# Attention on one core: the products of probabilities and values on half arrays, one step later

## The reference, cut to what matters

```
def _gqa(q, k, v):
    scale = 1.0 / np.sqrt(q.shape[-1])
    scores = jnp.einsum('bsghd,btgd->bghst', q, k) * scale
    p = jax.nn.softmax(scores, axis=-1)
    return jnp.einsum('bghst,btgd->bsghd', p, v)
```

## Time and profile before

| | |
|---|---|
| median of 3 runs (lowest, highest) | 1151.28 us (1149.92, 1151.87) |
| the profiled execution, its own time | 1148.86 us |
| its span, first to last instruction | 1147.0 us |
| self attention, first to last matmul of the stage | 282.3 to 645.7 us |
| cross attention, the same | 662.1 to 1058.7 us |
| busy share of the span | PE 78%, PEld 72%, DVE 79%, ACT 65%, POOL 34% |

### The profile page before, as it was taken

The page is one execution under the profiler, slowest core; times in us unless marked ns, Lnnn a source line. Parts: engine busy times, 40 slices in busy tenths (PEclk is TensorE's granted clock), DMA queues, the critical chain, the costliest instruction groups (busy, mean ns, idle before and its releaser), DMA issues. The chain is left out here.

```text
span 1147.0 us, 22788 instructions
## 1 busy us (share of the span) xinstructions
PE 898.3 (78%) x6366; PEld 820.7 (72%) x6366; DVE 909.2 (79%) x2442; ACT 746.6 (65%) x2599; POOL 393.1 (34%) x500
## 2 busy tenths in 40 slices
PE   3720066621999999999999379999999999997738
PEld 3620033321899999999999269999999999996627
DVE  7989989877788888888888458888888888886461
ACT  3445034363888888888888457777777777775303
POOL 0008910000244444444443543333334333333024
PEclk9855569755999999999999789999999999999559
DMA  6021200001100000000000210000000000000400
GB/s 223 1 92 57 72 0 1 0 0 64 48 2 1 0 0 0 0 0 0 0 0 0 79 50 5 6 10 5 5 5 5 9 5 5 0 0 1 152 19 19
DMA packets 18265, 26.94 MB, mean 23 GB/s; under 512 B 1264, under 2 KB 15408, under 8 KB 17456
## 3 DMA queue, kind: packets, MB, share of 16 engines
q1 hardware_dynamic: 17840, 25.41, 6.5%
q0 software_dynamic: 384, 1.05, 0.3%
HBM read 23.83 MB, written 2.62 MB: 23 GB/s over the span
## 5 line engine op out<-in xcount | busy, mean ns | idle before, releaser
L1208 POOL TENSOR_TENSOR c_cat<-c_tb,c_mb 128x512 fp32r<-128x512 bf16 x64 | 74.7, 1167 | 228.9 <-DVE c_tb L1286 228.9
L1208 POOL TENSOR_TENSOR s_cat<-s_tb,s_mb 128x512 fp32r<-128x512 bf16 x64 | 74.3, 1161 | 178.6 <-DVE s_tb L1286 178.6
L1384 ACT ACTIVATE c_p<-c_kT_sc_ps,c_nmax 128x64 f32<-128x64 f32 x256 | 76.8, 312 | 79.4 <-DVE c_nmax L1252 79.4
L1384 ACT ACTIVATE s_p<-s_kT_sc_ps,s_nmax 128x64 f32<-128x64 f32 x256 | 76.8, 312 | 39.6 <-DVE s_nmax L1252 39.6
L1401 PE MATMUL s_q_ps<-wq,s_xqf 128*128 128x512 f32 x256 | 76.7, 422 | 32.9 <-POOL s_xqf L1190 32.9
L1401 PE MATMUL c_q_ps<-wq,c_xqf 128*128 128x512 f32 x256 | 76.8, 423 | 16.4 <-DVE wv L645 16.4
L1455 PE MATMUL s_pj_ps<-wp,s_cat 128*128 128x256 f32 x512 | 77.7, 294 | 2.9 <-POOL s_cat L1208 2.9
L1455 PE MATMUL c_pj_ps<-wp,c_cat 128*128 128x256 f32 x512 | 77.2, 293 | 2.9 <-POOL c_cat L1208 2.9
L1245 DVE TENSOR_REDUCE c_v<-c_sq 128x6 f32<-128x768 f32 x64 | 61.0, 953 | 16.2 <-ACT c_sq L1355 15.1
L1401 PEld LDWEIGHTS s_q_ps<-wq,s_xqf 128*128 128x128 f32 x256 | 44.3, 193 | 39.2 <-POOL s_xqf L1190 33.3
L1479 PEld LDWEIGHTS s_kT_sc_ps<-s_kT,s_qT 128*128 128x128 f32 x512 | 66.6, 191 | 7.4 <-ACT s_qT L1360 1.4
(11 more groups left out here) (361 smaller groups left out, 2985.0 us busy)
## 6 DMA issues: line engine op xcount, KB each, us to landing
x_res<-in_x SPq DMA_DIRECT2D x4, 512.0 KB, 5.4
vT<-in_ctxT SPq DMA_DIRECT2D x2, 1024.0 KB, 9.9
tf_work<-in_wqT SPq DMA_DIRECT2D x2, 1024.0 KB, 6.2
tf_work<-in_wprojT SPq DMA_DIRECT2D x2, 1024.0 KB, 5.4
w_work<-in_wqxT SPq DMA_DIRECT2D x2, 1024.0 KB, 6.6
w_work<-in_wkvxT SPq DMA_DIRECT2D x2, 1024.0 KB, 8.1
c_ctx<-in_ctxT SPq DMA_DIRECT2D x16, 128.0 KB, 2.3
w_work<-in_wprojT SPq DMA_DIRECT2D x2, 1024.0 KB, 5.7
```

Source lines behind the costliest of these rows:

```text
L1208: nc.gpsimd.tensor_tensor(cat[out8.o % 2][:], tb[:], mb[:], ALU.subtract).then_inc(cat_ready, 1)
L1384: nc.scalar.activation(pe_s[:, a * S:(a + 1) * S], sc_ps[:, a * S:(a + 1) * S], ACT.Exp, bias=nmax[:, a:a + 1], accum_out=psum_s[:, a:a + ...
```

## The change

The products with the values are computed for each sequence by itself. `pT` now holds only the blocks themselves (128 partitions x 256), written by one copy. For each group and each sequence, one matmul contracts over the 64 partitions of that sequence, 128 columns wide; partitions 0 to 63 lie on one half of the array's rows, 64 to 127 on the other. The two sequences write into two PSUM banks. No bank is free for that: a tensor `qo_ps` of three banks now holds, in its outer banks, the two query buffers, and in its middle one the old `po_ps`; the products of a unit go to the middle bank and to one of its neighbours (`out_banks`). So they wait until the normalised queries have been read out of that neighbour (`qn_ready` at pv.n + 3), and the queries that are next written there wait until the products have been read (`y_ready`).

The step of these products is one later on PE (unit u-4 instead of u-3), and the orders within a step change on PE, DVE and ACT. One constant of the first stage (`K_BOUND`, the value in a shift of exponents) is another number; it changes no instruction.

```
-        pT = sb("pT", [P, GU, HPG, 2, S])
+        pT = sb("pT", [P, GU * P])
-        q_ps = [psum(f"q_ps{i}", [P, QW]) for i in range(2)]
+        qo_ps = psum("qo_ps", [P, 3, 512])
+        q_ps, po_ps = [qo_ps[:, 2 * i, :] for i in range(2)], qo_ps[:, 1, :]
-        po_ps = psum("po_ps", [P, 512])
+        def out_banks(u):
+            return qo_ps[:, u.o % 2:u.o % 2 + 2, 0:HU * S]
@@ @block.gpsimd @@
-                nc.gpsimd.memset(pT[:], 0.0).then_inc(cleared, 1)
@@ @block.vector, step @@
+                    if f8.live:
+                        round8(3)
                     if sm.live:
                         maxima()
-                    if f8.live:
-                        round8(3)
                     if u.live:
                         normalised()
+                    if pv.live:
+                        dve.wait_ge(pv_done, pv.count(1, 1))
...
+                        nc.vector.tensor_tensor(yb[:].rearrange("p (h b s) -> p h b s", h=HU, b=2),
+                                                out_banks(pv).rearrange("p b (h s) -> p h b s", h=HU),
...
                     if sm.live:
                         dve.wait_ge(exp_ready, sm.count(4, 4))
                         wait_unit(dve, pn_ready, sm.before(1))
                         nc.vector.reciprocal(rsum[:], psum_s[:]).then_inc(rsum_ready, 1)
-                    if pv.live:
...
@@ @block.scalar, step @@
-                    u, sm, pv = units(i, o, 0, 1, 2)
+                    q, u, sm, pv = units(i, o, 0, 1, 2, 3)
...
-                        for b in range(2):
-                            rows = slice(b * S, (b + 1) * S)
-                            nc.scalar.activation(pT[rows, :, :, b, :], po_ps[rows, 0:GU * P].rearrange(
-                                "p (g h s) -> p g h s", g=GU, h=HPG), ACT.Copy).then_inc(pT_ready, 1)
+                        nc.scalar.activation(pT[:], po_ps[:, 0:GU * P], ACT.Copy).then_inc(pT_ready, 1)
...
+                    if q.live:
+                        act.wait_ge(q_done, q.count(1, 1))
+                        wait_unit(act, var_ready, q.before(1))
+                        nc.scalar.activation(sq[:, 0:QW], q_bank(q), ACT.Square).then_inc(sqq_ready, 1)
@@ @block.tensor, step @@
-                    u, kv_u, t, pv, pj = units(i, o, 0, 1, 2, 3, 5)
+                    u, kv_u, t, pt, pv, pj = units(i, o, 0, 1, 2, 3, 4, 5)
...
+                    if pv.live:
+                        pe.wait_ge(pT_ready, pv.count(1, 1))
+                        pe.wait_ge(qn_ready, min(pv.n + 3, UNITS) if pv.static else pv.count(1, 3))
+                        for g in range(GU):
+                            for b in range(2):
+                                rows = slice(b * S, (b + 1) * S)
+                                last = nc.tensor.matmul(out_banks(pv)[:, b, g * P:(g + 1) * P],
+                                                        v_s[pv.o % 4][rows, g * D:(g + 1) * D],
+                                                        pT[rows, g * P:(g + 1) * P], start=True, stop=True)
+                        last.then_inc(pv_done, 1)
...
+                        wait_unit(pe, y_ready, u.before(4))
...
-                        for g in range(GU):
-                            last = nc.tensor.matmul(po_ps[:, g * HPG * P:(g + 1) * HPG * P],
-                                                    v_s[pv.o % 4][:, g * D:(g + 1) * D],
-                                                    pT[:, g].rearrange("p h b s -> p (h b s)"), start=True, stop=True)
-                        last.then_inc(pv_done, 1)
```

More of the change, by code:

```diff
@@ L1084, in attention_stage @@
     ROUNDS = NT // 2
+    UNITS = WIDTH * ROUNDS
     QW, KW = HU * D, GU * D
@@ L1386, in step @@
                                                  ).then_inc(exp_ready, 1)
-                pipeline(act, step, ROUNDS, WIDTH, 2)
+                pipeline(act, step, ROUNDS, WIDTH, 3)
             @block.tensor
@@ L1438, in step @@
                         last.then_inc(tq_done, 1)
-                        pe.wait_ge(kn_ready, t.count(1, 1))
-                        wait_unit(pe, kT_ready, t.before(1))
-                        wait_unit(pe, exp_ready, t.before(1, 4))
-                        for a in range(GU):
-                            last = nc.tensor.transpose(kT_ps[:, a * P:(a + 1) * P], kn[:, a * P:(a + 1) * P], ident[:])
-                        last.then_inc(t_done, 1)
                     if pj.live:
@@ L1459, in step @@
                         last.then_inc(pj_done, 1)
-                    if pv.live:
-                        pe.wait_ge(pn_ready, pv.count(1, 1))
-                        wait_unit(pe, y_ready, pv.before(1))
-                        for g in range(GU):
-                            last = nc.tensor.transpose(po_ps[:, g * P:(g + 1) * P], pn[:, g * P:(g + 1) * P], ident[:])
-                        last.then_inc(pt_done, 1)
+                    if t.live:
+                        pe.wait_ge(kn_ready, t.count(1, 1))
+                        wait_unit(pe, kT_ready, t.before(1))
+                        wait_unit(pe, exp_ready, t.before(1, 4))
+                        for a in range(GU):
+                            last = nc.tensor.transpose(kT_ps[:, a * P:(a + 1) * P], kn[:, a * P:(a + 1) * P], ident[:])
+                        last.then_inc(t_done, 1)
                     if u.live:
@@ L1470, in step @@
                         wait_unit(pe, qn_ready, u.before(2))
-                        split_product(q_bank(u)[:], lambda h: xqf[tp][:, h, :], wq, gp * QW, (gp + 1) * QW
+                        wait_unit(pe, y_ready, u.before(4))
+                        split_product(q_bank(u), lambda h: xqf[tp][:, h, :], wq, gp * QW, (gp + 1) * QW
                                       ).then_inc(q_done, 1)
+                    if pt.live:
+                        pe.wait_ge(pn_ready, pt.count(1, 1))
+                        wait_unit(pe, y_ready, pt.before(1))
+                        for g in range(GU):
+                            last = nc.tensor.transpose(po_ps[:, g * P:(g + 1) * P], pn[:, g * P:(g + 1) * P], ident[:])
+                        last.then_inc(pt_done, 1)
                     if t.live:
```

26 lines of the change are left out of this document (8 added, 18 removed).

## The result

| | before | changed |
|---|---|---|
| median (lowest, highest) | 1150.95 us (1149.92, 1151.87), 4 runs | 1182.38 us (1179.81, 1185.25), 4 runs |
| the profiled execution, its own time | 1148.86 us | 1184.29 us |
| its span | 1147.0 us | 1182.6 us |
| mean step, self attention | 5.453 us | 5.785 us |
| mean step, cross attention | 5.907 us | 6.051 us |

The changed kernel takes 1.0274 times as long, 95% interval [1.0244, 1.0304]: 31 us slower. The prediction was 1174.5 us, range 1138 to 1222, with 0.74 for slower.

A forecast was written before the change was run, and what follows sets the result against it. PE's own work was taken to set the step before the change. Self attention +24.3, cross attention +0.6 and POOL's clearing -0.5 made +24.4 us; on 1148.86 that is 1173.3, with half of 2.4 added 1174.5 us, range 1138 to 1222.

The forecast's parts named there:

- The new wait: PE's products wait for DVE's qn of the unit two ahead, which puts them in series with DVE's step.
- Side by side: Products on the two array halves overlap, the second half starting one record late: 0.55 us, between 0.44 and 0.88.
- p: Time of the products with the values a step: 0.55 + 0.15 = 0.70 us, ends 0.54 and 1.08, against 0.92 before.
- The way back: PE's switch from 64 rows back to 128 after the products: 0.15 us, between 0.10 and 0.20.
- the first loop: Self attention: from qn through products, yb, s_r, tb and maxima back to qn; 5.07 us + p with the x_res addition.
- the second loop: Self attention: ACT's ln and exp behind kT, behind PE's moved key transposes; 5.16 us + p with the x_res addition.
- Self attention: Step 5.12 + 0.70 = 5.82 us against 5.44: +0.38, times 64 = +24.3 us.
- Cross attention: Step 5.92 us against 5.91, with 0.10 for the statistics: +0.6 us in all.
- 1: Rival: the array halves take turns, p = 1.03, self step 6.15, cross 6.25; 1217 us; chance 0.28.
- 2: Rival: the products halve to p = 0.46 and the switches vanish in the waits; 1144 us, faster; chance 0.08.
- 3: Rival: the loops are shorter than their parts and PE stays the bound; 1121 or 1136 us; chance 0.10.
- 4: Rival: it comes out even, p = 0.54 to 0.60 and a fixed part 0.1 shorter; within 0.2%; chance 0.08.

The follow-up runs named there:

- e1: Changed kernel with its new orders, but whole-array products into the old middle bank alone and without the two bank waits; 1150.47 us, 0.9993 of before.
- e2: e1 with the changed kernel's two bank waits (on qn_ready and y_ready) kept; 1213.74 us, 1.0552 of before.
- e8: Changed kernel, second sequence's products in the transposed queries' bank; PE does queries before transposes, ACT copies kT before qT; 1158.70 us, 1.0060 of before.
- e5: Changed kernel with both groups' products of the lower array half written ahead of those of the upper half; 1182.72 us, 1.0271 of before.
- e3: Changed kernel with PE's transposes of the keys right behind those of the queries, ahead of the projection; 1169.51 us, 1.0172 of before.
- e10: Changed kernel with DVE's addition into x_res moved behind kn, ahead of yb, and the statistics behind rsum; 1165.00 us, 1.0119 of before.
- e11: Changed kernel with GpSimd's conversions treating only 8 of a tile's 128 tokens from the third tile on; 1177.96 us, 1.0238 of before.
- e9: e8 with whole-array products into po_ps alone and no wait for another bank; 1158.88 us, 1.0064 of before.
- e4: e3 with DVE's tb moved from ahead of the maxima to behind kn; 1226.99 us, 1.0666 of before.
- e6: Changed kernel with DVE writing qn ahead of the maxima, which stand between qn and kn; 1167.65 us, 1.0136 of before.
- e7: Changed kernel with the altered orders of e3, e6 and e10 together; 1159.15 us, 1.0069 of before.

## Why the prediction was right, point by point

The sign and the cause were right, and the time lies within the range. The sum was +24.4 us and the two profiled executions are 35.5 apart: self attention 5.1 below its figure, cross attention 9.5 above, between and behind the stages 6.7 above. That the self attention's figure is so near is in part luck, as the third point shows.

- **The new wait** was the mechanism, and PE's products now stand in series with DVE's step. e1, e2 and e8 show it: the waits added to e1 cost 63 us, and e8, with half arrays and without that wait, has TensorE's own step in the self attention (5.455, against 5.453 before).
- **Side by side** was right as far as the records tell, and its length was mis-sized. p was 0.55 + 0.15 from "five places instead of four"; there are four, and in e5 the order changes nothing. But they are not evenly spaced: the second place starts 0.21 behind the first and the others 0.11, with a stop in front (454.44) and without one (805.88, 806.10, 806.21, 806.32). The way back costs 0.15 in front of transposes (last product's end to the first transpose's, 0.26 by the records, less their pace of 0.11). That is the value that I took.
- **The loops.** The 5.83 of the step shown must not be set against the prediction's mean of 5.82, since it has a conversion in it. A plain step was to be 5.65 by the first loop and 5.74 by the second, and is 5.66, by terms that erred against each other. Products after a stop 0.72 for p + 0.22 = 0.92, because the way back lies behind the hand-over to DVE and was counted within it; hop from PE to DVE 0.04 (455.16 to 455.20) for 0.14; `yb` to `s_r` 3.29 in the plain step (455.20 to 458.49) for 3.11, and 3.53 beside the conversion (449.37 to 452.90). That stretch is longer because of the second loop: DVE waits for ACT's `g` in nearly every step, because the late `kT` is in front of it. The two loops don't take turns; they are interlaced, and e3 shows that the second was worth 13 us. The third, through the scores and the maxima, was not in the prediction at all. It sets the floor of 5.66 in both attentions, 0.07 above what the other two leave in that step, and it limits what e3 and e10 give back.
- **Self attention**: expected +0.38 a step, measured +0.33. The sum +24.3 us was +19.2. Over four steps the mean is 5.66, plus 0.07 for the addition (a step of 5.93; 0.12 in the prediction), plus 0.05 for GpSimd's conversion (a step of 5.85 in the mean; not in the prediction), plus 0.01 for one step of 5.76 in eight. The missing term nearly makes up for the two that were too large.
- **Cross attention**: expected +0.01, measured +0.14 a step, 10.1 us for 0.6. This is the term that was mis-sized. Four steps in a row last 6.18, 5.66, 6.67 and 5.76. The 6.67 has the addition and the statistics, from 810.01 to 810.99, 0.98 for the 0.90 in the prediction; it adds 0.25 to the mean step, for 0.22. The 6.18 has GpSimd's conversion and subtraction, which add 0.41 to `c_t`; it adds 0.13, and the prediction had nothing for it. That one term is the miss; the plain step was even 0.04 shorter than predicted (5.66 for 5.70). Neither can be had back whole: e10 makes the 6.67 and e11 the 6.18 into 5.83, PE's own work, and a short step behind becomes 5.83 too, so that they bring 0.178 and 0.041 of a mean step back.
- **Between the stages**: expected -0.5, measured +4.3 and +1.9 behind the last. e1, with the same depth, has 44.2 between them, so 1.8 go with the deeper pipeline and its orders. The other 2.5 are open: e2, with both waits, has 44.4, and e3, with the keys' transposes early, 44.6. I had priced no filling and draining at all. What I had added for the median, 1.2 us, was immaterial.
- **Clock and ACT.** The granted clock was 1.00 and 0.99 in the two windows. ACT was right: the moved squares cost nothing (e1). e1 has the two copies of `pT` again, so for the single copy it says nothing; e8, which has it, takes as long as e9, which has not.
- **The rivals.** 1 falls with the pairs: eight records start within 0.44 us and not 0.88. e5 alone would not decide it, since halves that took turns would not care for the order either. 2 had the products nearly right, with the loops' rest too short and the switches wrongly gone. 3 and 4 fall with PE's wait for `qn` in 61 of 64 units of the self attention; in the cross attention it waits in 15 of 64, and PE's own work does bind some steps. The whole-array products of e1 take 0.87 from start to start (810.25 to 811.12) and four pairs 4 x 0.105 = 0.42; of these 0.45 only 0.07 remain, so entry and exit together take 0.38, an estimate from these differences. The Trainium skill, TensorEngine Tiling (Array Packing), Theoretical Speedup, gives up to 2x for such tiles, and Key Properties a drain at each change of mode: the records agree with both as far as eight records in four places and the time lost at entry and exit go, and here the second leaves little of the first.

## What to carry to other kernels

A buffer borrowed from a neighbour in the pipeline is a wait, and its price is the whole path between the two uses on both engines, to be summed along the timeline before the faster instruction is counted; here it was 63 us with whole arrays, and with half arrays the kernel was still 31 us slower than before, against a possible gain of 9. When an order is changed to relieve a loop, follow the moved instruction's consumers on every engine (`tb` to `cat` to the projection, the maxima to the exponentials to the squares), since e3, e4, e6 and e7 each met a new wait there. Test the idea with the wait taken away (another bank, or whole arrays) before tuning the orders around it.

## What the runs showed of the hardware that was not expected

- The eight records of a half-array group start in four pairs whatever the order of the halves in the program: one half's products ahead of the other's (e5) took the same time as alternating ones, 1182.7 and 1182.4 us.
- What a half-array group saves depends on its neighbours: 0.07 us a step in front of 128-column transposes (one step of e1 against one of the changed kernel), 0.02 in front of 512-column queries (e8 and e9). With whole arrays the group that follows starts 0.68 behind the products in e9 and 0.87 in e1.
- Two of VectorE's operations on 128x6 elements are held until an instruction of GpSimd that started before them ends: in the changed kernel `s_v` runs from 451.01 to 451.78 and GpSimd's conversion from 450.93 to 451.76; `c_t` from 821.66 to 822.24 and GpSimd's subtraction from 821.50 to 822.22:

```profile
450.93 0.83 POOL L1195 CAST s_xqf<-xq 128x768 fp32r x1
```

```profile
821.66 0.58 DVE L1266 SCALAR_TENSOR_TENSOR c_t<-c_g 128x6 f32<-128x6 f32 x1 [0.50 <-ACT c_g L1371]
```

```profile
821.50 0.72 POOL L1200 TENSOR_TENSOR c_ctxp<-c_ctx,c_ctxp 128x256 fp32r<-128x256 f32 x1
```

The Trainium skill, SBUF — State Buffer, Who interferes with whom, states that the two engines share a pair of ports, which for some of VectorE's instructions one of the engines holds for a whole instruction while the other is blocked. These rows agree, in that the small operation ends 0.02 us after GpSimd's; no run here shows the port itself. With nearly all of the conversions left out the kernel is 4.4 us faster (e11).
